# A two-block first gate part, second experts block by block with PSUM summing, and a cast moved to GpSimd

## The reference, cut to what matters

```python
def _gate(x2, gate_w, gate_b):            # 16 experts in 8 groups of 2
    scores = sigmoid(x2 @ gate_w.T)
    s = (scores + gate_b).reshape(T, G, E // G)
    group_scores = top_k(s, 2)[0].sum(-1)
    top_groups = top_k(group_scores, 4)[1]          # 4 of 8 groups for every token
    ...
    idx = top_k(masked s, 8)[1]                     # so both experts of each chosen group
    w = scores at idx; w = w / w.sum() * 2.5

def _moe_forward(x, ...):
    pos = running count of each expert's tokens, in token order
    xb = zeros((E, CAP, DIM)).at[flat_e, pos].set(x, mode='drop')   # CAP = 256
    h = silu(xb @ w1) * (xb @ w3)
    y = (h @ w2) gathered back, 0 for dropped tokens, times w, summed over the 8
```

```
after 1 block:   493  103  266  197   79  362   93  455
after 2 blocks:  992  194  536  379  167  738  188  902
after 3 blocks: 1485  289  817  566  246 1120  264 1357
after 4 blocks: 1973  385 1091  762  333 1485  343 1820
```

## Time and profile before

| | before |
|---|---|
| median of 3 runs | 1411.34 us (1411.24 to 1416.61) |
| the profiled execution's own time | 1410.25 us |
| its span, first to last instruction | 1408.4 us |
| mean granted TensorE clock | 0.914 |
| busy share PE / DVE / ACT / POOL | 78 / 59 / 53 / 39 % |

### The profile page before, as it was taken

The page is one execution under the profiler, slowest core; times in us unless marked ns, Lnnn a source line. Parts: engine busy times, 40 slices in busy tenths (PEclk is TensorE's granted clock), DMA queues, the critical chain, the costliest instruction groups (busy, mean ns, idle before and its releaser), DMA issues. The chain is left out here.

```text
span 1408.4 us, 32619 instructions
## 1 busy us (share of the span) xinstructions
PE 1103.4 (78%) x9950; PEld 731.9 (52%) x9951; DVE 825.5 (59%) x1640; ACT 744.3 (53%) x1748; POOL 546.3 (39%) x401
## 2 busy tenths in 40 slices
PE   6869787665602999999999989965999999965586
PEld 2324344332302988888888888862444444422354
DVE  3653345443525555555555555542899999984576
ACT  5855397655711555555555555544666666622364
POOL 0000006555570322322322222232799999991000
PEclk9989899888755999999999999998999999985599
DMA  6100001331122111111111111112111111101000
GB/s 202 47 1 0 1 1 54 112 129 52 33 67 62 44 39 37 38 38 37 37 38 38 38 37 37 38 31 82 30 30 60 60 60 60 46 30 77 0 1 30
DMA packets 60525, 65.22 MB, mean 46 GB/s; under 512 B 9841, under 2 KB 50301, under 8 KB 60336
## 3 DMA queue, kind: packets, MB, share of 16 engines
q1 hardware_dynamic: 49616, 46.47, 11.3%
q0 software_dynamic: 8832, 17.00, 3.7%
q10 hardware_dynamic: 2016, 0.94, 0.2%
HBM read 37.12 MB, written 28.55 MB: 47 GB/s over the span
## 5 line engine op out<-in xcount | busy, mean ns | idle before, releaser
L921 DVE SCALAR_TENSOR_TENSOR m_hl<-ps,m_hh 128x512 f16<-128x512 f32 x292 | 200.4, 686 | 158.2 <-ACT m_hh L893 155.9
L801 POOL DMA_INDIRECT expert_out<-m_result,m_token x148 | 144.5, 976 | 377.8 <-DVE m_result L933 374.1
L893 ACT ACTIVATE m_hh<-ps 128x512 f16<-128x512 f32 x292 | 174.2, 596 | 179.0 <-PE ps L854 176.7
L836 PE MATMUL ps<-m_x,weights 128*128 128x128 f16 x1168 | 212.8, 221 | 44.5 <-ACT m_x L887 43.7
L838 PE MATMUL ps<-m_x,weights 128*128 128x128 f16 x1168 | 211.7, 220 | 0.0
L837 PE MATMUL ps<-m_x,weights 128*128 128x128 f16 x1168 | 211.7, 220 | 0.0
L745 POOL DMA_INDIRECT dispatched<-d_rows,slot x128 | 128.4, 1003 | 211.6 <-DVE slot L647 126.2
L851 PE MATMUL ps<-weights,m_hh 128*128 128x128 f16 x1160 | 209.2, 219 | 0.0
L853 PE MATMUL ps<-weights,m_hl 128*128 128x128 f16 x1160 | 209.2, 219 | 0.0
L852 PE MATMUL ps<-weights,m_hh 128*128 128x128 f16 x1160 | 209.2, 219 | 0.0
L1043 POOL TENSOR_TENSOR iv_pool_sum<-iv_pool_sum,iv_pool_part 128x1024 f32<-128x1024 f32 x80 | 188.6, 2358 | 12.1 <-DVE iv_pool_part L1258 3.8
(11 more groups left out here) (306 smaller groups left out, 2238.0 us busy)
## 6 DMA issues: line engine op xcount, KB each, us to landing
m_rows<-dispatched SPq DMA_DIRECT2D x152, 65.5 KB
X<-x SPq DMA_DIRECT2D x16, 512.0 KB, 4.3
iv_got<-expert_out SPq DMA_DIRECT2D x16, 512.0 KB, 4.3
out<-X SPq DMA_DIRECT2D x16, 512.0 KB, 3.0
Y<-w_moe SPq DMA_DIRECT2D x8, 512.0 KB
expert_out<-m_result,m_token POOLq DMA_INDIRECT x148, 2.2
dispatched<-d_rows,slot POOLq DMA_INDIRECT x128
Y<-w_last SPq DMA_DIRECT2D x1, 2048.0 KB
```

What stands on the lines that cost most here:

```text
L801: pool.indirect_dma_start(env.yt, bass.IndirectOffsetOnAxis(ap=token[:, k:k + 1], axis=0), result[:, k, :], None, bounds_check=TOKENS - 1, ...
L836: pe.matmul(out, high, xh, start=True, stop=False)
L893: act.activation(hh[e][:, :], hidden[e], ACT.Relu).then_inc(hi_ready[e], 1)
L921: dve.scalar_tensor_tensor(hl[e][:, :], hidden[e], 0.0, hh[e][:, :], ALU.max, ALU.subtract).then_inc(h_split[e], 1)
```

## The change

FIRST_BLOCKS goes from 4 to 2, so the involution sends images 1 to 15 and leaves out only image 0. The spreading matrix is rounded by GpSimd, in the gate phase. After the gate, DVE reduces `need` to its maximum over the groups and keeps it between 2 and 32 as `served`, one number instead of nine. The second experts run over blocks 0 to `served`-1, and in each block over all eight groups, open or not (the weights of a full group's tokens are zero). The eight `down` matmuls of a block half accumulate in one PSUM bank, and DVE adds to X once per half and block. Waits and signals are per bank: `up` waits before A, before B and before the spread separately, with one semaphore where there were three. SP sends a block of 512 tokens as soon as it is added. One semaphore `passed` stands in place of one per engine.

```diff
-FIRST_BLOCKS = 4
+FIRST_BLOCKS = 2
...
@@ phase_gate1
+        @block.gpsimd
+        def _(pool):
+            pool.wait_ge(S["w_loaded"], 16 * len(weight_loads))
+            pool.tensor_copy(env.spread[:, :, :], env.spread32[:, :, :]).then_inc(S["w_ready"], 1)
...
             blocks(dve, body, last=decide)
-            dve.wait_ge(S["w_loaded"], 16 * len(weight_loads))
-            dve.tensor_copy(env.spread[:, :, :], env.spread32[:, :, :])
-
             link = chain(dve, S["cleared"])
-            link(dve.tensor_scalar(need[:, :], need[:, :], float(BLOCKS), None, ALU.min))
-            link(dve.tensor_tensor_scan(room[:, :], need[:, :], env.eps[:, 2:3].broadcast_to([P, G1]), 0.0, ALU.add, ALU.add))
-            link(dve.memset(env.served[:, 0:1], 0))
-            link(dve.tensor_copy(env.served[:, 1:G1 + 1], room[0:1, :]))
-            link(dve.tensor_scalar(env.finals1[:, :], room[0:1, :], -1.0, None, ALU.add))
-
-            link(dve.tensor_copy(env.sends[:, 0:1], ends[0:1, 1:2]))
+            link(dve.tensor_reduce(least[0:1, 0:1], need[0:1, :], AX.X, ALU.max))
+            link(dve.tensor_scalar(env.served[:, 0:1], least[0:1, 0:1], float(BLOCKS), float(FIRST_BLOCKS), ALU.min, ALU.max))
...
@@ phase_experts1
         def _(sp):
-            last = sp.value_load(served[0:1, G1:G1 + 1], min_val=G1, max_val=G1 * BLOCKS)
-            wait_apart(sp, S["x_done"], last * 2 + 2, env.passed["sp"])
-            count = sp.value_load(env.sends[0:1, 0:1], min_val=FIRST_IMAGES, max_val=IMAGES)
+            count = served(sp)
             with sp.Fori(0, count) as n:
-                sp.dma_start(out[:, bass.ds(n * PIX, PIX)], image(X, n)).then_inc(S["sent"], 16)
+                sp.wait_ge(S["x_done"], n * 2 + 4)
+                sp.dma_start(out[:, bass.ds(n * BLOCK, BLOCK)], X[:, bass.ds(n * BLOCK, BLOCK)]).then_inc(S["sent"], 16)
...
+            def up(j, g, q, n):
+                pe.wait_ge(S["mid_ready"], j * 3 + 1)
+                pe.matmul(A[q], env.w1[:, g, :], cols(XN, n, q), start=True, stop=True).then_inc(S["up_ready"], 1)
+                pe.wait_ge(S["mid_ready"], j * 3 + 2)
+                pe.matmul(B[q], env.w3[:, g, :], cols(XN, n, q), start=True, stop=True).then_inc(S["up_ready"], 1)
+
+            def down(j, g, q, n):
+                pe.wait_ge(S["mid_ready"], j * 3 + 9)
+                if g == 0:
+                    pe.wait_ge(S["x_done"], n * 2 + q + 1)
+                pe.matmul(y[q], env.w2[:, g, :], h[q][:, :], start=(g == 0), stop=(g == G1 - 1)).then_inc(S["down_ready"], 1)
+
+            count = served(pe)
             up(0, 0, 0, 0)
-            for g, (first, final) in enumerate(group_steps(pe)):
-                with maybe_loop(pe, first, final) as i:
-                    step(i, g, (i - first) % BLOCKS, g, (i - first + 1) % BLOCKS)
-
-                step(final, g, (final - first) % BLOCKS, min(g + 1, G1 - 1), 0)
+            with pe.Fori(0, count) as n:
+                spread(n * per_block, 0, 0, n)
+                for k, (g, q) in enumerate(units):
+                    j = n * per_block + k
+                    if k + 1 < per_block:
+                        up(j + 1, *units[k + 1], n)
+                        spread(j + 1, *units[k + 1], n)
+                    else:
+                        up(j + 1, *units[0], (n + 1) % BLOCKS)
+                    down(j, g, q, n)
...
+            count = served(dve)
+            with dve.Fori(0, count) as n:
+                for k, (g, q) in enumerate(units):
+                    middle(n * per_block + k, q)
+                add(n, 0)
+                add(n, 1)
```

More of the change, by code:

```diff
@@ L1004, in _ @@
                 reload(n, n % 2)
-            reload(FIRST_IMAGES + 1, 1)
-            send(FIRST_IMAGES)
-            with by_two(sp, FIRST_IMAGES + 2, IMAGES - 2) as n:
+            with by_two(sp, FIRST_IMAGES + 1, IMAGES - 2) as n:
                 for q in range(2):
@@ L1548, in phase_experts1 @@
         A, B, spread_w, y = ([env.psum[i][:, q * HALF:q * HALF + UNIT1] for q in range(2)] for i in range(4))
+        units = [(g, q) for g in range(G1) for q in range(2)]
+        per_block = len(units)
         block = ctx.enter_context(nc.Block())
@@ L1552, in cols, with served @@
             return buf[:, bass.ds(n * BLOCK + q * UNIT1, UNIT1)]
[L1554 to L1557 removed]
+        def served(engine):
+            return engine.value_load(env.served[0:1, 0:1], min_val=FIRST_BLOCKS, max_val=BLOCKS)
         @block.sync
         def _(sp):
[L1561 to L1563 removed]
+            count = served(sp)
@@ L1596, in _ @@
             act.preload_act_table_set("natural_log_exp_and_others")
-            last = act.value_load(served[0:1, G1:G1 + 1], min_val=G1, max_val=G1 * BLOCKS)
-            with act.Fori(0, last) as i:
-                for q in range(2):
-                    j, s = i * 2 + q + 1, sig[q]
-                    act.wait_ge(S["a_ready"], j)
-                    act.activation(s[:, :], A[q], ACT.Exp, scale=-1.0).then_inc(S["exp_ready"], 1)
-                    act.wait_ge(S["exp_ready"], j)
-                    act.activation(s[:, :], s[:, :], ACT.Ln, bias=env.ones32[:, 0:1], scale=1.0).then_inc(S["softplus_ready"], 1)
-                    act.wait_ge(S["softplus_ready"], j)
-                    act.activation(s[:, :], s[:, :], ACT.Exp, scale=-1.0).then_inc(S["sig_ready"], 1)
+            count = served(act)
@@ new lines, in _ @@
+            with act.Fori(0, count) as n:
+                for k, (g, q) in enumerate(units):
+                    j, s = n * (per_block * 3) + k * 3, sig[q]
+                    act.wait_ge(S["up_ready"], j + 1)
+                    act.activation(s[:, :], A[q], ACT.Exp, scale=-1.0).then_inc(S["sig_steps"], 1)
+                    act.wait_ge(S["sig_steps"], j + 1)
+                    act.activation(s[:, :], s[:, :], ACT.Ln, bias=env.ones32[:, 0:1], scale=1.0).then_inc(S["sig_steps"], 1)
+                    act.wait_ge(S["sig_steps"], j + 2)
+                    act.activation(s[:, :], s[:, :], ACT.Exp, scale=-1.0).then_inc(S["sig_steps"], 1)
@@ L1627, in add @@
-            def add(j, q, n):
-                dve.wait_ge(S["down_free"], j + 3)
-                dve.tensor_tensor(cols(X, n, q), cols(X, n, q), y[q], ALU.add).then_inc(S["x_done"], 1)
-            def step(i, n, n_before):
-                hidden(i, 0)
-                if n_before is not None:
-                    add(i * 2 - 1, 1, n_before)
-                hidden(i, 1)
-                add(i * 2, 0, n)
-            n_before = None
-            for first, final in group_steps(dve):
-                step(first, 0, n_before)
-                with maybe_loop(dve, first + 1, final + 1) as i:
-                    step(i, (i - first) % BLOCKS, (i - first - 1) % BLOCKS)
-                n_before = (final - first) % BLOCKS
@@ new lines, in add @@
+            def add(n, q):
+                dve.wait_ge(S["down_ready"], n * per_block + (per_block + 1 + q))
+                dve.tensor_tensor(cols(X, n, q), cols(X, n, q), y[q], ALU.add).then_inc(S["x_done"], 1)
+            count = served(dve)
+            with dve.Fori(0, count) as n:
+                for k, (g, q) in enumerate(units):
+                    middle(n * per_block + k, q)
+                add(n, 0)
+                add(n, 1)
+            wait_apart(dve, S["x_done"], count * 2 + 2, env.passed)
@@ L1695, in build @@
             env.spread = sb3("spread", [P, G1, P], BF16)
-            env.served, env.sends = sb3("served", [1, G1 + 1], I32), sb3("sends", [1, 1], I32)
-            env.finals1 = sb3("finals1", [1, G1], I32)
+            env.served = sb3("served", [1, 1], I32)
             phase_gate1(nc, env, a)
```

61 lines of the change are left out of this document (24 added, 37 removed).

## The result

| | before | after |
|---|---|---|
| median | 1411.29 us (1410.61 to 1416.61, 4 runs) | 1761.53 us (1757.96 to 1765.27, 4 runs) |
| ratio | | 1.2472, 95% interval 1.2427 to 1.2516 |
| profiled execution, its span | 1410.25, 1408.4 us | 1758.7, 1756.8 us |
| mean granted clock | 0.914 | 0.849 |

What follows compares the result with a forecast made beforehand. Gate and experts were taken as chains of waits, so loop turns count. 283.1 + 2.0 + 65.3 + 1.2 - 1.3 - 2.9 - 1.2 = +346.2 us gave 1757 us; range 1698 to 1785, likeliest case 1745 to 1772.

Steps and rivals of the forecast that it cites:

- The count of passes: Gate and second experts: gate from 4 blocks to 32, experts from 16 steps to 32; 33 xs, 64 exponentials, 8 adds.
- The gate's 20.22 us for two blocks: Gate loop: each turn of two blocks takes 20.22 us, fourteen more turns, +283.1 us.
- The rival of a rising clock: Gate: full clock in all 28 blocks, -59 us, 1698 us; chance 0.22 that it takes off more than 12 us.
- The restart between the parts: Between the two gate parts: every engine waits for decide and reads ends again, +2.0 us, between 0 and 4.
- The experts: Second experts: 32 more units of 64 at 2.04 us each, +65.3 us; bounds +63.4 and +67.8.
- the rival: Second experts: a unit becomes dearer, by register instructions or instruction stream, 0.35 us on 64 units, 1779 us; 0.08 for over 1772.
- Block ends: Second experts: DVE adds both halves at each block's end, 0.3 us for each of 4 blocks, +1.2, up to 7.
- the register loads: Start of the second experts: eight DVE register loads put 2.9 us on the path, one load does not, -2.9 us.
- Waits per bank start nothing earlier: Second experts: PE issues A of the next unit only behind down, so per-bank waits gain nothing.
- The saved instructions: Between gate and experts: DVE's cast and six small instructions take 1.66 us, two small ones remain, -1.3 us.
- The tail: End of the kernel: one issue less and half as many bytes to send, -1.2 us, between -0.5 and -2.5.
- GpSimd's cast: Gate: the cast on GpSimd is hidden, 0 us; +2.4 once if it blocked DVE for its whole length.

Runs made afterwards that it cites:

- The run that stops after two blocks: The changed kernel with the second gate part always empty and served held at 2, leaving out tokens of blocks 2 and 3: 1297.74 us, ratio 0.9774.
- the filler run: The changed kernel with 5, 14 and 5 extra small bf16 matmuls in PE's waits of each gate block: 1656.44 us.
- the runs with an empty second part: The changed kernel with FIRST_BLOCKS = 4, 1385.84 us; and the changed kernel with second gate part always empty and served held at 2, 1297.74 us.
- the run with only the gate: The kernel before with FIRST_BLOCKS = 2 and the number of images sent set to the constant 2, experts group by group: 1610.37 us, ratio 1.2136.
- the fastest kernel above: The kernel before with the cast on GpSimd, PE issuing A and B two units ahead of down, and extra matmuls in the gate: 1306.78 us, ratio 0.9841.

## Why the prediction was right, and where it was off

**The count of passes** was right: 33 `xs`, 64 exponentials, 8 adds. It rests on `need` having the sum 16, on the 2,048 places of the first 512 tokens, and on the fact that every group must be full before the gate may stop. The run that stops after two blocks shows the other side of the same threshold.

**The gate's 20.22 us for two blocks** held over 14 more turns, and alone in the kernel before it gives 282.8. The rival of a rising clock was false: 0.50 over 335 us with PE busy for 225 of them. The sentence in the Trainium skill ("TensorE: Matmul & The Clock Gate", "The HAM clock gate") that sustained activity lifts the clock is not contradicted: without fillers the granted clock stayed at 0.50 throughout, and in the filler run it rose in places.

**The restart between the parts** was priced at 2.0 and took 1.4, but the step failed in another way: I added it and did not take off the pass over the empty second part, with its load, its branch and its second decision, which stood at the gate's end before. It is the 2.0 us by which the runs with an empty second part are longer from the last `xs` to A (7.6 and 7.7 against 5.7), and the 2.2 by which the run with only the gate is shorter there than before (6.24 against 8.42). So the restart is a move of that pass, worth 1.4 - 2.0 = -0.6, and not +2.0: 2.6 of the 3.4 us by which the sum was too high.

**The experts** came to +63.7, the sum of the terms to +63.6, and that is luck: errors in it cancel. The step is 4.13 us and not the 4.08 of the price. The prediction had looked at PE's register instructions and put them at zero; what shows is DVE's, about 0.19 us a step in the part from first multiply to down, against 0.35 a unit in the rival. Block ends took 0.4 to 0.6, not 0.3. In return the first step went from 8.40 to 4.22 us, 4.2 saved where 2.9 was priced for the register loads. The clock is in that too: it was still 0.50 in the stretch 1335 to 1338 before, 5 to 8 us behind the first A, and 1.00 from 1621 after, 4 us behind it; no run parts the two. Some 0.9 us more are saved in the last step, from its first exponential to the end of the last add (6.7 us before, 5.8 after).

**Waits per bank start nothing earlier** was right for this order of PE, in which A of the next unit is issued behind down. It says nothing against such waits: together with another order they were worth 38 us of 64 units.

**The saved instructions** (-1.3) gave -0.6. Of the -2.7 between the last `xs` and A, 2.1 are the empty pass (its two decisions start 1324.79 and 1326.88). The cast and the small instructions did go, from 1.66 us to 0.33; but from DVE's last one to A it is now 1.32 us instead of 0.60, with PE's load of `served` in it. The prediction took the one register load that is left as hidden, which it is on DVE and is not on PE.

**The tail** (-1.2, between -0.5 and -2.5) gave -2.7, outside its own bounds. One send of 256 KB lands in 2.0 us and one issue of 0.34 us lies ahead of it, where two issues took 1.19 and landing up to 3.1; and the issue starts 0.18 us behind the last add, where before it was 0.90.

**GpSimd's cast** was put at zero, and it is zero, but not because there is no lock. The trace after shows the cast and the DVE instruction beside it, and that instruction over all its 32 executions:

```profile
1293.36 1.14 POOL L1357 CAST spread<-spread 128x1024 bf16<-128x1024 f32 x1 [14.92 <-DMA e_w<-w_moe]
1293.63 1.14 DVE L1476 TENSOR_TENSOR g_above<-g_above,g_tie 128x256 f32<-128x256 f32 x1
```

```profile
L1476 DVE TENSOR_TENSOR g_above<-g_above,g_tie x32: 424/425/1141, 1293.6 to 1607.5; 128x256 f32<-128x256 f32 x32
```

The addition, with two SBUF inputs, takes 0.424 us each time but this once, 1.141, and it ends 0.27 us behind the cast. The same instruction is as long in six of the other eight kernels with this cast; in the fastest kernel above, the cast falls on the comparison `g_tie<-g_group`, also with two SBUF inputs, which takes 1.11 instead of 0.42 us, and in the filler run on `g_selected<-g_place`, 0.45 instead of 0.18. The Trainium skill says in "SBUF — State Buffer", "SBUF: two separate sides", that the one that starts second is blocked. The trace agrees but for the end: behind the cast's end only 0.27 us are left, less than the 0.42 that the addition takes. The price is 0.72 us, once, and DVE's idle time before the next `xs` takes it (0.27 us left of 0.96 in the earlier trace rows). The interval from that `xs` to the one before is 8.72, and 8.73 before the change.

**The rest.** 1757 against 1761.5 is close partly by luck. The sum was 3.4 too high for the last stretch, and what lies ahead of it made the medians 7.4 us more apart, which no term had; on the other chips the same difference is 339.9, and the sum 6.3 too high. All of this is well inside the range, and the mechanism, 28 more gate blocks and 32 more units, is as predicted.

## What to carry to other kernels

When a loop's number of turns depends on data, work out the number first; one threshold (167 tokens against 256) was worth more here than all instruction costs together. A stop that is tested earlier saves only if it can be met there, and failing it must not mean running to the end: by the gate's price, 20.22 us for two blocks, a second test two blocks later would have kept 14 turns away; that version wasn't run. Of a finer wait, look at the issue order of the engine before you price it: in one order it left the chain of a step as it was, and with another order 38 us were gone.

## What was unexpected of the hardware

- Fillers lifted the granted clock to 0.67 over most stretches of the gate and left its two large matmuls at 2.0 us each there, with no gain; only in the few blocks where these ran in 1.1 to 1.8 us did the gate get shorter.
- Two register instructions of 0.04 us each between DVE's multiplies of 0.42 us go with starts 0.545 us apart, where it was 0.455 without them.
- The same program is 85 us shorter on other chips, in the routing and the first experts, where tokens move by DMA; the last stretch of the changed kernel is 475.1 and 475.0 us on two of them.
- A 128x1024 cast from f32 to bf16 takes 1.04 to 1.21 us on GpSimd in these runs and 0.69 on DVE.
